# A Mamba-2 decoder layer on Trainium2: the state-space stage written without loops, its decay exponents formed by VectorE from rows spread by DMA

## The reference, cut to what matters

```
H, P, N, G, K, CH = 32, 128, 128, 8, 4, 32         # heads, head width, state, groups, taps, chunk
gate, hbc, dt = split(x @ in_proj_w.T)
hs, B, C = split(silu(causal_conv4(hbc) + conv_b))
dt = softplus(dt + dt_bias);  A_bt = -exp(A_log) * dt
A_cum = cumsum(A_bt)
Y[l] = sum over s <= l of (C[l] . B[s]) * exp(A_cum[l] - A_cum[s]) * dt[s] * X[s]  +  D * X[l]
y = rmsnorm_per_group(Y * silu(gate)) * norm_w;  out = y @ out_proj_w.T
```

## Time and profile before

| | |
|---|---|
| median of 3 runs | 2147.5 us |
| the profiled execution: its time, its span | 2146.56 us, 2144.8 us |
| mean granted TensorE clock | 0.978 of full speed |
| front | 0 to 177 us |
| state_space | 177 to 1076 us |
| middle, attention, output | 1076 to 2145 us |

### The profile page before, as it was taken

One profiled execution on the slowest core, in us unless ns is written; L12 is line 12 of the kernel. 1 busy time (PEld: TensorE's weight loads), 2 busy tenths in 40 slices (PEclk: granted clock), 3 DMA queues, 4 the chain that ended last, 5 costly groups with the idle time before them and its releaser, 6 DMA issues. The chain is left out here.

```text
span 2144.8 us, 37991 instructions
## 1 busy us (share of the span) xinstructions
PE 1803.8 (84%) x12364; PEld 1273.8 (59%) x12514; DVE 1649.4 (77%) x2759; ACT 1665.4 (78%) x2987; POOL 580.7 (27%) x482
## 2 busy tenths in 40 slices
PE   6987999999999999999967677777777777774999
PEld 4775878787878787878746333333333333333887
DVE  5886686767686767676888699999999999994443
ACT  4666888888888888888826899999999999994211
POOL 2001555555555555555510000100000100003000
PEclk8998999999999999999989999999999999997999
DMA  4000000000000000000082499999999999995000
GB/s 139 16 6 30 0 30 0 29 0 29 0 29 0 29 0 29 0 26 4 0 182 39 78 182 183 185 184 184 180 185 185 183 183 180 186 186 122 11 11 20
DMA packets 566249, 173.94 MB, mean 81 GB/s; under 512 B 535168, under 2 KB 558592, under 8 KB 566144
## 3 DMA queue, kind: packets, MB, share of 16 engines
q1 hardware_dynamic: 566144, 172.57, 42.8%
HBM read 27.83 MB, written 2.10 MB: 14 GB/s over the span
## 5 line engine op out<-in xcount | busy, mean ns | idle before, releaser
L1223 ACT ACTIVATE levels<-s_ps,nb,qstep 128x512 int16<-128x512 f32 (+1 forms) x768 | 695.8, 915 | 32.7 <-DVE nb L1188 31.7
L1178 DVE TENSOR_REDUCE mx<-s_ps 128x1 f32<-128x512 f32 (+1 forms) x768 | 630.8, 862 | 26.4 <-PE s_ps L1128 26.4
L1128 PE MATMUL s_ps<-kT,qT 128*128 128x512 bf16 x1447 | 445.6, 386 | 200.1 <-ACT levels L1223 181.2
L603 DVE SCALAR_TENSOR_TENSOR xs<-x_ps,cw,xs 128x508 f32<-128x508 f32 (+2 forms) x393 | 291.2, 741 | 174.3 <-ACT xs L525 135.9
L1128 PEld LDWEIGHTS s_ps<-kT,qT 128*128 128x128 bf16 x1532 | 107.8, 97 | 434.8 <-ACT levels L1223 383.7
L659 POOL TENSOR_TENSOR hid<-y,sg 128x512 f32<-128x512 f32 x128 | 175.2, 1369 | 277.7 <-ACT sg L547 185.1
L494 PE MATMUL o_ps<-wo,hid 128*128 x1024 | 242.8, 380 | 4.9 <-DVE acc L590 4.9
L494 PEld LDWEIGHTS o_ps<-wo,hid 128*128 128x128 f32 x1024 | 192.7, 189 | 39.5 <-issue 9.8
L525 ACT ACTIVATE xs<-x_ps,cb,cw 128x512 f32<-128x512 f32 x131 | 101.9, 777 | 116.1 <-PE x_ps L446 116.1
L1246 POOL TENSOR_TENSOR sum_part<-sums 128x16 f32<-128x16 f32 x16 | 3.4, 211 | 689.5 <-ACT levels L1223 689.5
L1136 PEld LDWEIGHTS ao_ps<-vi,levels_T 128*128 128x128 f16 x4096 | 139.9, 96 | 66.9 <-DMA levels_T<-levels 7.6
(11 more groups left out here) (201 smaller groups left out, 3255.2 us busy)
## 6 DMA issues: line engine op xcount, KB each, us to landing
w_raw<-winT_dram SPq DMA_DIRECT2D x18, 512.0 KB, 4.5
wo_raw<-woutT_dram SPq DMA_DIRECT2D x9, 512.0 KB, 5.7
kT<-zeros SPq DMA_DIRECT2D x4, 1024.0 KB, 18.7
qT<-zeros SPq DMA_DIRECT2D x4, 1024.0 KB, 16.1
levels_T<-levels SPq DMA_TRANSPOSE x256, 4.6
acc<-xT_dram SPq DMA_DIRECT2D x4, 512.0 KB, 5.5
w_bc<-winT_dram SPq DMA_DIRECT2D x16, 128.0 KB, 2.4
acc<-x_dram SPq DMA_DIRECT2D x1, 2048.0 KB, 11.1
```

Source lines behind the costliest of these rows:

```text
L603: dve.scalar_tensor_tensor(to, x_ps[:, :, 0:SEQ - s], cw[:, head, TAPS - 1 - s], to, ALU.mult, ALU.add).then_inc(chain if s < TAPS - 1 els ...
L1128: return pe.matmul(s_ps[:, BANKS[h % 2][chunk], :], qT[:, qt, h, :], kT[:, h, at:at + GT], start=True, stop=True)
L1178: dve.tensor_reduce(mx[:, u, at:at + 1], src, AX.XY if what == "cd" else AX.X, ALU.max).then_inc(max_done, 1)
L1223: act.activation(levels[:, s, at:at + banks * GT].rearrange("p (c k) -> p c k", c=banks), s_ps[:, bank:bank + banks, :], ACT.Exp, bias=nb[ ...
```

## The change

Four edits, all in the mixer.
- `state_space` has no hardware loop. A Python loop writes out all 128 units with constant addresses and semaphore values. The added increments of `held` go, and so do the preparation of weights behind the last group, the projections behind the last unit, and the two PSUM memsets.
- `front` leaves the running sums in float32: one copy, four transposes, one copy, and four DMAs that write them to a DRAM tensor `rows` of one row per head. The one-hot tile and the bf16 mask go.
- In `state_space` SP issues one DMA per unit, which reads a head's 512 running sums and spreads them to all 128 partitions of one of four buffers `row`. The two `d_ps` matmuls go. In their place DVE forms min(row - cum, mask) with four instructions of 128 x 128 per unit (`exponent`), behind `mix` in its slot. ACT takes exp of the whole unit in one instruction, in place.
- `x_ps` has two buffers, in the PSUM bank that `d_ps` leaves and its own.

```diff
@@ front: SP
+                if j == 4:
+                    sp.wait_ge(cum_copied, 1)
+                    for b in range(BG):
+                        sp.dma_start(mem["rows"].rearrange("h (q b l) -> h q b l", q=TG, b=BG)[:, :, b, :],
+                                     cumT[b * H:(b + 1) * H, :, :]).then_inc(mem["rows_stored"], 16)
@@ front: POOL
-            pool.tensor_copy(mask[:, :], maskf[:, :]).then_inc(extra, 1)
-            pool.tensor_copy(onehot[:, :, :], sel[:, :].unsqueeze(2).to_broadcast([PARTS * H, H, P])).then_inc(extra, 1)
@@ front: DVE
-                    dve.tensor_copy(parts[:, :, 0, :], cum_ps).then_inc(chain, 1)
...
-                    dve.tensor_tensor(parts[:, :, 2, :], rest[:, :, :], parts[:, :, 1, :], ALU.subtract).then_inc(parts_done, 1)
+                    dve.tensor_copy(cum[:, :, :], cum_ps).then_inc(parts_done, 1)
@@ state_space: SP
-            with sp.Fori(0, G) as g:
-                sp.wait_ge(w_ready, g * HG + HG)
-                load((g + 1) % G)
+            sp.wait_ge(mem["rows_stored"], 16 * BG)
+            for n in range(UNITS):
+                r, h, g, tg, head = place(n)
+                if n >= RING:
+                    sp.wait_ge(d_ready, n - RING + 1)
+                sp.dma_start(row[:, n % RING, :, :].rearrange("p b l -> p (b l)"),
+                             mem["rows"][head:head + 1, tg * GT:(tg + 1) * GT].partition_broadcast(P)
+                             ).then_inc(row_loaded[n % RING], 16)
+                if n % (TG * HG) == TG * HG // 2 and g + 1 < G:
+                    load(g + 1)
@@ state_space: PE
-                    pe.wait_ge(conv_done, n)
-                project(x_ps, 0, n, r, h, x_ready)
+                        pe.wait_ge(conv_done, n - 2 + 1)
+                    project(x_ps[:, n % 2, :, :], 0, n, x_ready)
-                    pe.matmul(d_ps[:, :, :], onehot[:, bass.ds(head_of(r, h), 1), :],
-                              cumT[:, bass.ds(r % TG * GT, GT)], start=True, stop=False)
-                    pe.matmul(d_ps[:, :, :], identb[:, :], mask[:, :], start=False, stop=True).then_inc(d_ready, 1)
@@ state_space: ACT
-                    for b in range(BG):
-                        ex = act.activation(decay[:, h % 2, b, :], d_ps[:, b, :], ACT.Exp,
-                                            bias=ncum[:, bass.ds(r % TG * BG + b, 1), bass.ds(head_of(r, h), 1)])
-                    ex.then_inc(decay_ready, 1)
+                    act.activation(decay[:, n % 2, :, :], decay[:, n % 2, :, :], ACT.Exp).then_inc(decay_ready, 1)
@@ state_space: DVE
+            def exponent(n):
+                r, h, g, tg, head = place(n)
+                dve.wait_ge(row_loaded[n % RING], (n // RING + 1) * 16)
+                if n > 1:
+                    dve.wait_ge(mix_ready, n - 1)
+                for b in range(BG):
+                    ins = dve.scalar_tensor_tensor(decay[:, n % 2, b, :], row[:, n % RING, b, :],
+                                                   ncum[:, tg * BG + b, head:head + 1], mask[:, :], ALU.add, ALU.min)
+                ins.then_inc(d_ready, 1)
...
+            dve.wait_ge(nw_loaded, 16)
+            exponent(0)
+            for h in range(HG):
+                rest_of_weights(0, h)
+            for m in range(-LEAD, UNITS):
+                if m >= 0 and m // HG % TG == TG - 1 and m // (HG * TG) + 1 < G:
+                    rest_of_weights(m // (HG * TG) + 1, m % HG)
+                if m > 0 and m % HG == 0:
...
+                    finish(m // HG - 1)
...
                     dve.tensor_tensor(mix[...], decay[...], gs[...], ALU.mult).then_inc(mix_ready, 1)
+                n = m + 3
+                if 0 < n < UNITS:
+                    exponent(n)
```

More of the change, by code:

```diff
@@ L198, in _ @@
                     pe.wait_ge(parts_done, 1)
[L199 to L202, removed]
+                    for q in range(TG):
+                        tr = pe.transpose(ct_ps[:, q, :], cum[:, q * BG:(q + 1) * BG, :].rearrange("p b h -> p (b h)"),
+                                          mem["ident"][:, :])
                     tr.then_inc(ct_done, 1)
@@ L501, in slot @@
                                            start=(b == 0), stop=(b == BG - 1), skip_group_check=True)
-                    mm.then_inc(out_unit, 1)
-            for hh in range(HG - LEAD, HG):
-                slot(-1, hh, False)
-            with pe.Fori(0, ROUNDS) as it:
-                for hh in range(HG):
-                    slot(it, hh, True)
+                    mm.then_inc(out_done, 1)
         @block.scalar
@@ new lines, in _ @@
+            dve.memset(ones[:, :], 1.0).then_inc(consts, 1)
+            dve.memset(half[:, :], -0.5).then_inc(consts, 1)
+            dve.wait_ge(nw_loaded, 16)
+            exponent(0)
+            for h in range(HG):
+                rest_of_weights(0, h)
+            for m in range(-LEAD, UNITS):
+                if m >= 0 and m // HG % TG == TG - 1 and m // (HG * TG) + 1 < G:
+                    rest_of_weights(m // (HG * TG) + 1, m % HG)
+                if m > 0 and m % HG == 0:
+                    if m == HG:
+                        dve.wait_ge(acc_loaded, 16)
+                        dve.wait_ge(consts, 2)
+                    finish(m // HG - 1)
+                n = m + 3
+                if n < UNITS:
+                    r, h, g, tg, head = place(n)
+                    dve.wait_ge(tap_ready, n + 1)
+                    for s in range(1, TAPS):
+                        if s > 1:
+                            dve.wait_ge(conv_chain, n * 2 + (s - 1))
+                        to = xs[:, h, :, s:]
+                        dve.scalar_tensor_tensor(to, x_ps[:, n % 2, :, 0:SEQ - s], cw[:, head, TAPS - 1 - s:TAPS - s], to,
+                                                 ALU.mult, ALU.add).then_inc(conv_chain if s < TAPS - 1 else conv_done, 1)
+                n = m + 2
+                if 0 <= n < UNITS:
+                    r, h, g, tg, head = place(n)
+                    if n > 1:
@@ L671, in _ @@
-            factor(ROUNDS)
+            pool.wait_ge(consts, 2)
+            for n in range(UNITS):
+                r, h, g, tg, head = place(n)
+                if h == 0 and r:
+                    factor(r - 1)
+                pool.wait_ge(yd_ready, n + 1)
+                pool.wait_ge(sg_ready, n + 1)
+                pool.tensor_tensor(hid[:, n % 2, :, :], y[:, n % 2, :, :], sg[:, n % 2, :, :],
+                                   ALU.mult).then_inc(hid_ready, 1)
+                pool.wait_ge(hid_ready, n + 1)
+                if h == 0:
+                    if r:
+                        pool.wait_ge(out_done, r * HG)
+                    pool.tensor_tensor(ssum[:, :, :], hid[:, n % 2, :, :], hid[:, n % 2, :, :], ALU.mult).then_inc(sq_ready, 1)
+                    continue
+                pool.tensor_tensor(sq[:, :, :], hid[:, n % 2, :, :], hid[:, n % 2, :, :], ALU.mult).then_inc(sq_chain, 1)
+                pool.wait_ge(sq_chain, r * (HG - 1) + h)
+                pool.wait_ge(sq_ready, n)
+                pool.tensor_tensor(ssum[:, :, :], ssum[:, :, :], sq[:, :, :], ALU.add).then_inc(sq_ready, 1)
@@ L674 @@
+            factor(ROUNDS - 1)
 MAGIC = 1.5 * 2.0 ** 23
```

275 lines of the change are left out of this document (100 added, 175 removed).

## The result

The changed kernel takes 2315.67 us (median of 4 runs, 2315.21 to 2318.39) against 2147.45 for the kernel before in the same comparison (2143.91 to 2147.55): **1.0793 times as long, 95% interval 1.0776 to 1.081**, or 168 us more. The forecast was 2228, inside a range that ended at 2335. The sign and the mechanism came as predicted, and the sum took the wrong one of two orders of events, which lay some hundredths of a microsecond apart.

A forecast was written before the change was run, and what follows sets the result against it. PE was taken as the bound before, DVE after the change. Profiled execution 2146.56, plus 79 in the state-space stage, plus 1 for row DMAs and front, gave 2226.6; the runs' median lies 0.9 higher: 2228 us, range 2150 to 2335.

The forecast's parts named there:

- DVE and POOL exclude each other for whole instructions, and the exponents meet it: State-space stage: DVE instructions with two SBUF tensors, such as the exponents, and POOL's hid, sq, ssum wait for each other.
- What comes next after the first exponent: DVE slot after hid: second exponent beats POOL's sq, two exponents per gap, slot 6.83 us, total 2228; chance 0.42.
- the comparison of lead-ins: At hid's end: POOL asks for ports some 0.15 us after its start, DVE sooner, from wo's whole overhead of 0.14.
- the price of one exponent: DVE, one exponent of 128 columns alone: 0.29 us, standing 0.20 apart, 0.8 us per unit, 102 in all.
- the forecast's 28.2: Stage round without weights: three slots of 6.83 us, one of 4.86, and finish at 2.87.
- The rival with one per gap: DVE slot: sq and ssum get the ports first, slot 8.04 us, round 31.9, total 2323; chance 0.25.
- PE's saving buys nothing: Stage: PE loses two d_ps matmuls, 0.45 us per unit, 57.6 in all, but is no longer the bound.
- Row DMAs hidden by the ring: SP's 128 row DMAs cost nothing, asked for three slots ahead; only the stage's start pays, about +3 us.
- Front: Before the stage: at most four instructions of 512 columns go and dt loses 0.2: -2 us, between -3 and 0.
- The weights at 0.41 and 0.68: DVE's wo and w_lo with POOL idle, expected in the first weights slot; in the other three they wait, 2.03 us later.
- the eighth group: Stage: the useless eighth preparation of weights goes, leaving 7 rounds with weights at 35.2 us.
- `hid` behind the exponents: Faster rival in the stage: exponents pass before POOL's hid asks, 36 us less, 2112; chance 0.13.

The follow-up runs named there:

- pool_hid_only: Changed kernel with POOL's square and sum left out for three of four heads, only hid kept; output norm not the reference's: 2135.16 us.
- mask_bank: Changed kernel with the mask copied to a PSUM bank, given up by the second x_ps buffer, so exponents read one SBUF and one PSUM tensor: 2090.97 us.
- one_input: Changed kernel with the mask left out, each exponent reading one SBUF tensor; exponents above the diagonal are wrong: 2193.17 us.
- cols96: Changed kernel with exponents and exp covering only 96 of each 128 columns, the others left at a constant: 2213.68 us.
- unrolled_d_ps: Changed kernel's loop-free state-space, but front, d_ps matmuls on PE, four exp and single x_ps buffer as before, no row DMAs: 2115.71 us.
- mask_bank_w: mask_bank with the weights' DVE instructions wo and w_lo moved from the slot's start to behind xdt: 2082.6 us.

## Why the prediction was right and wrong

- **DVE and POOL exclude each other for whole instructions, and the exponents meet it: right.** The ends 0.15 and 0.16 us behind `hid`, `sq` and `ssum` show it, and `pool_hid_only` and `mask_bank` each remove it from one side and get 180 and 225 us back. As a condition "two SBUF tensors" was too narrow: a form with one waits as well (`one_input`).
- **What comes next after the first exponent: wrong, and this is the miss.** The step was "So I take it that the second exponent comes first: two exponents fit into a gap between POOL instructions." The recorded starts were forecast well: `sq` 0.08 and the second exponent 0.09 behind the end of `hid`, measured 0.08 and 0.07. What failed is the comparison of lead-ins, POOL's "some 0.15" against "DVE has less lead-in, as `wo`'s whole overhead is 0.14 (0.41 less 0.27)". It took the overhead of another form. An exponent takes 0.34 us alone, 0.31 with 96 columns and 0.28 with 64, so 128 columns are about 0.14 of it and the overhead is 0.20 or a little more. And DVE proves to be the later of the two: 0.01 us of lead in the starts is not enough (188 of 188), 0.04 is (`cols96`, 186 of 186). If the one that asks first gets the ports, an estimate follows: an exponent asks later behind its recorded start than POOL does, by 0.01 to 0.04 us, where the forecast had it earlier. Which part of the overhead this is stays open. The same overhead is missing in the price of one exponent, 0.29 for 0.34, and in the 0.20 from start to start, where (1.13 - 0.34) / 3 = 0.26 is measured.
- **What the step is worth.** 30 rounds are 4.0 us longer each than the forecast's 28.2, 120 in all; the weights cost 3.7 per group and not 7.0, 23 less; the last round is 22.3, 6 less. That makes 91, against 88 missed. With `cols96`, which falls on the other side, the round is 28.2, the weights 7.0, and the time 2214, near the forecast's 2228.
- **The rival with one per gap: came true.** It foresaw the ends of the exponents, counted from the end of `y`, at 1.90, 3.02, 4.38 and 4.58; they are 1.90, 3.02, 4.40 and 4.66. The round of 31.9 is 32.2; the weights' 3.7 us per group are 0.9 + 2.8 = 3.7, over two rounds (33.1 and 35.0); and its time of 2323 stands 0.3% above the 2316 measured. That closeness is in part luck: 30 rounds are 0.3 us longer than the rival's, 9 in all, and the last round, in which three of four slots have no taps and no exponents left, takes 22.3 and not 31.9, 10 less. It was held at 0.25 against 0.42. With a margin of some hundredths, and no row that tells which engine has the longer lead-in, the two should have been about even.
- **PE's saving buys nothing: right** for this kernel. PE needs about 24.3 us per round by the prediction, and once the waits are gone (`mask_bank`) the round takes 24.6. So 1.4 us of the 1.8 per round can be had (26.0 in `unrolled_d_ps`), and the changed kernel could not use them.
- **Row DMAs hidden by the ring: right.** DVE waits once, 3.56 us, at the stage's start, and the first `wo` starts 4.71 us behind DVE's first instruction of the stage and not 1.67: +3.0 as predicted. Front gives 2.5 where 2 was taken.
- **The weights at 0.41 and 0.68: right,** at 413 and 680 ns in the mean. Behind the four exponents POOL is done in every slot. The prediction had them wait in three of four, which belongs to the order that did not come; it did come with 96 columns, where a preparation costs 0.9 + 6.1 = 7.0 us.
- **No price for the loops: missed.** The sum had nothing for code without loops but the eighth group and the taps. `unrolled_d_ps` gains 30 us, 19 of them in the rounds. What the loops are worth in the changed kernel no run shows.
- **`hid` behind the exponents: not so,** as argued: `hid` starts at 565.49, ahead of the first exponent at 565.94.

## What to carry over

Before work is moved to DVE, look at what POOL does in that stretch: an instruction with two SBUF tensors, or a form with one tensor like that of `one_input`, costs its own time plus what is left of the POOL instruction that it meets, up to a whole one, and four short ones can cost nearly four times their work (4.14 us against 1.13). Put one operand in PSUM, move them to where POOL is idle, or join them into fewer instructions, in that order of gain here (2091, 2110 and 2264 us against 2316). Where a sum turns on which of two engines comes first by a few hundredths, give both orders and even chances, as a term that small can decide 100 us.

## What the runs showed of the hardware

- **The order of recorded starts does not by itself decide between DVE and POOL.** In the slot shown the second exponent is recorded at 567.24 and `sq` at 567.25, and `sq` went through in 1.04 us while the exponent took 1.20. The Trainium skill (SBUF — State Buffer, section "SBUF: two separate sides") gives the pair to the one that starts first. Whole instructions are indeed held off, but the trace does not agree on the order at a distance of 0.01 us, in 188 cases; at 0.04 (`cols96`) it does, in 186. What inside an instruction counts as its start is open.
- **A small step in length is a large step in time.** Four exponents take 2.66, 2.79 and 4.14 us beside POOL at 64, 96 and 128 columns in the slots shown, and 0.86, 1.00 and 1.13 with POOL idle.
- **A PSUM operand cost nothing here.** With the mask in PSUM four exponents take 1.11 us, with the mask in SBUF and POOL idle 1.13.
- **The granted clock fell with PE's work.** In the stretch from 500 to 600 us it is 0.93 in the changed kernel, so part of that stretch ran at 1.2 GHz, with PE 83.09 us busy and waiting for DVE in between; it is 1.00, 2.4 GHz, in `mask_bank_w` at 96.97. PE was not the bound in the former, so this has no share of its own in the 168 us that any run here shows.
